# Attention with its inverse sums in the units that turn p, and the end of a layer in passes of parts

## The chip, the cores and the metric

The kernel runs on one core of a Trainium2 chip. The metric is the device time of one execution in microseconds (us). A core has five engines that run side by side and wait for one another by semaphores: TensorE (PE in the profile; PEld is its weight load), VectorE (DVE), ScalarE (ACT), GpSimd (POOL) and SyncE (SP), which issues most transfers.

## The reference, cut to what matters

A graph network on 1250 nodes with 512 features and 40000 edges, four stages one after the other. The change touches the second stage, two layers of attention over edges with 8 heads of 64 features. Of each layer it computes

```
scores = einsum('ehd,ehd->eh', q[tgt], k[srcidx])
m = segment_max(scores, tgt);  p = exp(scores - m[tgt])
s = segment_sum(p, tgt)
w = p / (s[tgt] + 1e-16)
agg = segment_sum(w[:, :, None] * v[srcidx], tgt)
attn = agg.reshape(n, D) @ Wo[l].T + bo[l]
x = _batchnorm(x + attn, g1[l], beta1[l])
ff = relu(x @ W1[l].T + b1[l]) @ W2[l].T + b2[l]
x = _batchnorm(x + ff, g2[l], beta2[l])
```

with Wo 512 by 512, W1 256 by 512 and W2 512 by 256. The batch norm is over the 1250 nodes, for each feature.

## The kernel before, in words

Edges are not walked one by one. Each layer has two blocks of code, `attend` and `finish_layer`, and between blocks the engines meet.

**attend** works on dense tiles: 8 heads times 10 groups of 128 target nodes, 80 steps, each with the 1250 source nodes in a row. What an engine does in step n stands in its own loop, in an order written out by hand; steps are skewed (scores run three steps ahead). In one step PE makes the scores of one tile (6 matmuls, L1337 and L1338, into banks 0 to 2), DVE takes them out and adds the logarithms of the edge counts (L1435, which I call a take), ACT does the exponential and sums it (L1396), PE turns the tile in two units of five 128 by 128 transposes (L1355, banks 4 to 7), ACT and DVE split each unit into a high and a low part (L1404, L1441), and PE multiplies the parts with the values (L1366, L1367, bank 3). The scores have one set of banks, so the scores of the next tile wait for the take of this one. Two heads are a pair, 20 steps; there are four pairs.

After each pair the sum is inverted and spread over 64 columns per head (`invert`, L1451 to L1453, at the end of step 21, 41 and 61), PE transposes the ten blocks of it into the banks of the scores (`spread`, L1345), and DVE multiplies the pair's rows of the result with it out of these banks (`divide`, L1460). For the first three pairs this stands in the middle of the loop, one step after the inversion; for the last one behind it. The list `score_plan` puts the spreads among the scores, and the counter `taken` counts both. GpSimd meanwhile gathers edge features for a later stage, 28 groups per layer (L806, L809).

**finish_layer** loads and turns Wo, W1 and W2 (L1055, ACT copies them out, L1581). `product` (L1556) multiplies: for each of the outputs (512 or 256 features in blocks of 128, times three thirds of 417 nodes) it runs over all input blocks in float32, and four banks go round. DVE adds bias and the old x (L1643); after three thirds it has a block of 128 features complete, takes its mean and variance (L102 to L108), ACT gives the root (L1585), and DVE normalises (L1624 to L1631). Product n waits until sum n-4 is out of its bank. W1 waits at its first output for the blocks of x one by one (`x_ready`), and in layer 0 the weights Wq of the next layer are turned after its second output. ACT applies relu (L1598). W2 starts when all six thirds of the hidden layer are there. In layer 1 GpSimd adds a row to ten tiles as soon as x is normalised (L1530).

The same kernel does another product in three passes already: `project_tensor` (L1142) for q and k of a layer, where both sides are split into a high part that PE takes in its fast float32 format (fp32r) and the rest, and high x high, high x low and low x high are added up.

## Time and profile before

| what | us |
|---|---|
| median of 3 runs (lowest, highest) | 2629.24 (2628.74, 2633.49) |
| the profiled execution | 2624.77 |
| its span in the trace | 2622.6 |
| PE busy | 2421.7 (92%) |
| DVE busy | 2063.6 (79%) |
| ACT busy | 1701.0 (65%) |
| POOL busy | 1087.3 (41%) |

Times in the trace count from the start of the span. Layer 0 has its attend from 808 to 1113 and its finish from 1113 to 1208, layer 1 from 1287 to 1594 and from 1594 to 1682. In a row of the timeline stand: start, busy time, engine, line, operation, output <- input, how many were merged, and in brackets how long the engine was idle before and what ended that. A row of the windows has: stretch, length, then busy time and instructions of PE, PEld, DVE, ACT and POOL, the clock granted to TensorE (1.00 is 2.4 GHz, 0.50 is 1.2 GHz), the share of the DMA engines and GB/s. A group of lines has: line, engine, operation, output <- input, shapes, count | busy us, mean ns of one | idle before.

### The profile page before, as it was taken

To read this page: it belongs to the slowest core of one execution; us is meant where nothing else is said; L and a number is where in the kernel's file an instruction comes from. 1 tells how busy PE (TensorE), PEld (TensorE's weight loads), DVE (VectorE), ACT (ScalarE), POOL (GpSimd) and SP (SyncE) were. 2 spreads that over 40 slices of the span, in tenths; PEclk is the share of its full clock that TensorE was granted. 3 is DMA by queue.
4 is the path that set the end of the run, shared out by engine and by line. 5 is a ranking of instruction groups with operands and counts; after the bars stand their busy time and mean duration, and the time that the engine had idled before them with its cause. 6 is when DMAs were issued, how large, how long until landed. Compare 5 with 4: busy or idle time off the path is not lost. (4 is left out here: it accounts for less than half of the span.)

```text
span 2622.6 us, 44503 instructions
## 1 busy us (share of the span) xinstructions
PE 2421.7 (92%) x12795; PEld 1927.9 (74%) x12795; DVE 2063.6 (79%) x4105; ACT 1701.0 (65%) x3714; POOL 1087.3 (41%) x1059
## 2 busy tenths in 40 slices
PE   6999699998998999999999998788999999988987
PEld 3777455556798999857899995456777777757776
DVE  8789699998646888836498885666999999966767
ACT  1789788886725777614377772242999999945460
POOL 1776655534203544000154420213777777720122
PEclk9999899999999999999899999898999999998999
DMA  2004022213245344112444441113877777841101
GB/s 94 3 3 126 29 66 65 65 43 101 74 176 124 101 113 116 32 65 100 138 120 117 91 79 65 49 56 120 245 235 241 237 238 236 224 122 36 49 9 39
DMA packets 116544, 278.10 MB, mean 106 GB/s; under 512 B 23991, under 2 KB 38266, under 8 KB 116414
## 3 DMA queue, kind: packets, MB, share of 16 engines
q0 software_dynamic: 51328, 138.78, 19.3%
q1 hardware_dynamic: 65086, 137.65, 16.8%
q8 instruction: 73, 1.20, 0.2%
q14 instruction: 57, 0.47, 0.1%
HBM read 208.80 MB, written 59.43 MB: 102 GB/s over the span
## 5 line engine op out<-in xcount | busy, mean ns | idle before, releaser
L806 POOL DMA_INDIRECT feature_rows<-in_edge_attr,id_idx x352 | 341.0, 969 | 448.9 <-POOLq L1507 226.9
L2081 POOL DMA_INDIRECT x_got<-table_dram,src_idx x352 | 375.4, 1066 | 110.0 <-issue 82.6
L1441 DVE TENSOR_TENSOR pt_low<-bank,pt_high 128x640 fp32r<-128x640 f32 x320 | 262.8, 822 | 52.8 <-ACT pt_high L1404 51.6
L761 ACT ACTIVATE hot_rest<-hot_dst,slot_w 128x128 bf16<-128x128 bf16 x864 | 273.1, 400 | 44.1 <-DVE hot_dst L711 44.1
L1404 ACT CAST pt_high<-bank 128x640 fp32r<-128x640 f32 x320 | 219.6, 687 | 114.3 <-PE bank L1355 114.3
L2225 DVE TENSOR_TENSOR msg<-bank,x_got 128x512 f32<-128x512 f32 x352 | 236.9, 684 | 42.6 <-ACT msg_high L2170 15.6
L1435 DVE CUSTOM_DVE_ANT_0 p<-bank,log_counts 128x1254 f32<-128x1254 f32 x160 | 232.6, 1454 | 14.7 <-PE bank L1338 14.5
L1355 PE MATMUL bank<-ident,p 128*128 128x128 f32 x1600 | 229.1, 275 | 2.3 <-DVE pt_low L1441 2.3
L1396 ACT ACTIVATE p<-p,bound 128x1254 f32<-128x1254 f32 x160 | 215.3, 1346 | 9.8 <-DVE bound L1435 9.8
L1366 PE MATMUL bank<-pt_high,val 128*128 128x256 f32 x800 | 212.3, 300 | 0.9 <-DVE agg_t L1447 0.9
L2205 DVE SCALAR_TENSOR_TENSOR msg_low<-msg,msg_high 128x512 fp32r<-128x512 f32 x308 | 209.7, 681 | 0.0
L2170 ACT ACTIVATE msg_high<-msg 128x512 fp32r<-128x512 f32 x308 | 193.4, 628 | 14.6 <-DVE msg L2225 14.2
L217 POOL DMA_INDIRECT slots_dram<-rec,pos x152 | 154.4, 1015 | 113.3 <-issue 102.4
L1367 PE MATMUL bank<-pt_low,val 128*128 128x256 f32 x800 | 199.2, 284 | 0.0
L1355 PEld LDWEIGHTS bank<-ident,p 128*128 128x128 f32 x1600 | 190.7, 142 | 11.4 <-issue 3.2
L1337 PE MATMUL bank<-keys,queries 128*128 128x418 f32 x480 | 186.6, 389 | 12.6 <-DVE bound L1435 7.3
L1338 PE MATMUL bank<-keys,queries_low 128*128 128x418 f32 x480 | 172.7, 360 | 0.0
L782 PE MATMUL bank<-hot_src,hot_rest 128*128 128x417 bf16 x864 | 172.0, 341 | 0.0
L809 POOL DMA_DIRECT2D features_dram<-feature_rows x88 | 51.0, 580 | 275.8 <-DMA feature_rows<-in_edge_attr,id_idx 275.8
L582 PE MATMUL bank<-row_hot,col_part 125*128 125x352 f32 x840 | 157.2, 340 | 8.6 <-ACT col_part L625 4.5
L582 PEld LDWEIGHTS bank<-row_hot,col_part 125*128 125x128 f32 x840 | 135.9, 191 | 29.6 <-issue 20.1
L1366 PEld LDWEIGHTS bank<-pt_high,val 128*128 128x128 f32 x800 | 152.9, 191 | 1.3 <-DVE pt_low L1441 1.3
(439 smaller groups left out, 6336.4 us busy)
## 6 DMA issues: line engine op xcount, KB each, us to landing
features_dram<-feature_rows POOLq DMA_DIRECT2D x88, 256.0 KB
edge_got<-features_dram SPq DMA_DIRECT2D x88, 256.0 KB, 3.7
qk_dram<-qk_high SPq DMA_DIRECT2D x16, 640.0 KB, 2.9
qk_dram<-qk_low SPq DMA_DIRECT2D x16, 640.0 KB, 4.2
keys<-qk_dram SPq DMA_DIRECT2D x32, 320.0 KB, 4.7
queries<-qk_dram SPq DMA_DIRECT2D x32, 320.0 KB, 6.7
queries_low<-qk_dram SPq DMA_DIRECT2D x32, 320.0 KB, 8.7
acc_a<-zeros SPq DMA_DIRECT2D x1, 6400.0 KB, 31.1
```

The source lines that it names most:

```text
L582: m = pe.matmul(ps_p[:, q, :], col_part[0:EP, u, q, :], row_hot[0:EP, u, :], start=(c == 0), stop=(c == PE_COLS - 1))
L761: last = act.activation(hot_rest[:, u, j, q, :], hot_dst[:, u, :, j], ACT.Copy, scale=k.slot_w[:, 1 + q, bass.ds(tile0 + j, 1)])
L806: pool.indirect_dma_start(out=self.rows[:, u, t % GT * ED:(t % GT + 1) * ED], out_offset=None, in_=self.a.edge_attr_128, in_offset=bass.In ...
L1355: t = pe.transpose(unit(i)[:, j * P:(j + 1) * P], p[:, n % AHEAD, (u * HALF + j) * P:(u * HALF + j + 1) * P], k.ident[:])
L1366: pe.matmul(to, v, p_high[:, slot, j, :], start=(u == 0 and j == 0), stop=False)
L1396: act.activation(rows, rows, ACT.Exp, bias=bound[:, n % 4:n % 4 + 1], scale=-1.0, accum_out=sums[:, n // (2 * NB) % 2, n % NB, n // NB % 2 ...
L1404: act.copy(p_high[:, made % 3, :, n % 2 * P:(n % 2 + 1) * P], unit(2 * n + u).rearrange("p (j n) -> p j n", n=P)).then_inc(high_made, 1)
L1435: dve.tensor_tensor_reduce(out=thirds(p[:, n % AHEAD, :]), in0=k.bank[:, 0:3, 0:THIRD], in1=thirds(k.log_counts[:, n % NB, :]), scale=-1.0 ...
L1441: dve.tensor_tensor(p_low[:, made % 3, :, columns], unit(2 * n + u).rearrange("p (j n) -> p j n", n=P), p_high[:, made % 3, :, columns].bi ...
L2081: pool.indirect_dma_start(out=xg[:, g % XRING, j, :], out_offset=None, in_=k.table_dram, in_offset=bass.IndirectOffsetOnAxis(ap=k.src_idx[ ...
L2205: dve.scalar_tensor_tensor(low[:, u, j, :], msg[:, j, :], 0.0, high[:, u, j, :].bitcast(F32), ALU.max, ALU.subtract).then_inc(low_done, 1)
L2225: dve.tensor_tensor(msg[:, j, :], k.bank[:, 2 + j, :], xg[:, r, j, :], ALU.add).then_inc(added_x, 1)
```

## The change

1. In `attend` the inverse sums of the first three pairs no longer go through the banks of the scores. PE transposes them as two further units of five blocks in the ring of units that turns p, one behind step 24 (44, 64) and one behind step 25 (45, 65); ACT copies each to SBUF (`inv_rows`), and GpSimd multiplies the pair's rows with it, between two of its groups of edge features (`SCALED_BEHIND`). The last pair is done as before.
2. In `finish_layer` the products with Wo and W2 take three passes of parts in fp32r instead of one float32 product. ACT rounds the result of attention and the weights to the high part, DVE subtracts to get the low part. The first six outputs of Wo are run input block by input block, over six banks; the other six output by output.
3. W1 stays float32, with its six outputs in six banks, input block by input block. Half of Wq is turned before its last block and half behind it. ACT writes the hidden layer twice (rounded, and whole), DVE subtracts.

```
+SCALED_BEHIND = (30, 53, 76)
...
-        p = (n - (2 * NB + 5)) // (2 * NB)
-        if n >= 2 * NB + 5 and (n - (2 * NB + 5)) % (2 * NB) == 0:
-            plan.append(("spread", p))
-        plan.append(("scores", n))
-    plan.append(("spread", HP - 1))
+        behind = n - 2 * NB - SPREAD_BEHIND
+        for u in range(2):
+            plan.append(("p", n, u))
+            if behind >= 0 and behind % (2 * NB) in (0, 1) and u == 1:
+                plan.append(("inv", behind // (2 * NB), behind % (2 * NB)))
     return plan
...
-            features.gather(pool, GATHERED[l], GATHERED[l + 1])
+            first, end = GATHERED[l], GATHERED[l + 1]
+            for pair in range(HP - 1):
+                until = first + (end - first) * SCALED_BEHIND[pair] // BLOCKS
+                features.gather_groups(pool, first, until)
+                first = until
+                pool.wait_ge(inv_copied, 2 * (pair + 1))
+                pool.wait_ge(batch_added, 2 * HALF * (pair + 1))
+                rows = at.agg[:, pair, :]
+                pool.tensor_tensor(rows, rows, inv_rows[:].rearrange("p u n -> p (u n)"), ALU.mult).then_inc(pair_scaled, 1)
+            features.gather_groups(pool, first, end)
+            features.all_stored(pool, end)
...
+            def unit_free(item):
+                i = turn_of[item]
+                if i >= UNITS:
+                    kind, n, u = turns[i - UNITS]
+                    pe.wait_ge(low_made if kind == "p" else inv_copied, 2 * n + u + 1)
...
+            def turn_inverse(pair, u):
+                pe.wait_ge(inv_ready, pair + 1)
+                unit_free(("inv", pair, u))
+                for j in range(HALF):
+                    t = pe.transpose(unit(("inv", pair, u))[:, j * P:(j + 1) * P], spread_inv(pair)[:, u * HALF + j, :], k.ident[:])
                 t.then_inc(turned, 1)
...
                     turn(n, 0)
-                if n + AHEAD < BLOCKS:
-                    kind, i = next(following)
-                    if kind == "spread":
-                        spread(i)
-                        kind, i = next(following)
                 if n >= 2:
                     values((n - 2) // 2, n % 2)
                 if n < BLOCKS:
                     turn(n, 1)
                 if n + AHEAD < BLOCKS:
-                    scores(i)
+                    scores(n + AHEAD)
+                if n in inverse_behind:
+                    turn_inverse(*inverse_behind[n])
             spread(HP - 1)
...
+            def copy_inverse(pair, u):
+                act.wait_ge(turned, turn_of["inv", pair, u] + 1)
+                if pair:
+                    act.wait_ge(pair_scaled, pair)
+                act.copy(inv_rows[:, u, :], unit(("inv", pair, u))).then_inc(inv_copied, 1)
...
-                if n + AHEAD < BLOCKS:
-                    kind, i = next(following)
-                    if kind == "spread":
-                        divide(i)
-                        kind, i = next(following)
                 if n < BLOCKS:
                     low_part(n, 0)
                 if n >= 3 and n % 2 == 1:
...
-                if n > 1 and n % (2 * NB) == 1:
+                if n > 1 and n % (2 * NB) == INVERTED:
                     invert(n // (2 * NB) - 1)
                 if n + AHEAD < BLOCKS:
-                    take(i)
+                    take(n + AHEAD)
...
-                    if n >= 2:
+                    if 2 <= n < 2 + KC:
+                        pe.wait_ge(w_lowered, n - 1)
+                    elif n >= 2:
                         pe.wait_ge(w_copied, n - 1)
...
+            def rows_of_wo(n, i):
+                to, o, c = out_of(n, RING)
+                for q, s in ((0, 0), (0, 1), (1, 0)):
+                    m = pe.matmul(to, wo[:, q, i, o], agg_parts[s][:, i, c], start=(i == 0 and q + s == 0), stop=(i == KC - 1 and q == 1))
+                return m
 
             turn(0, KC)
-            pe.wait_ge(w_copied, KC)
-            product(wo, at.agg, KC, KC, o_done, o_added, None, lambda: turn(KC, len(turns)), OTHERS)
+            for i in range(KC):
+                pe.wait_ge(w_lowered, i + 1)
+                pe.wait_ge(agg_low_made, i + 1)
+                for n in range(RING):
+                    m = rows_of_wo(n, i)
+                    if i == KC - 1:
+                        m.then_inc(o_done, 1)
+            turn(KC, len(turns))
+            for n in range(RING, 3 * KC):
+                pe.wait_ge(o_added, n - RING + 1)
+                for i in range(KC):
+                    m = rows_of_wo(n, i)
+                m.then_inc(o_done, 1)
             pe.wait_ge(w_copied, len(turns))
-            pe.wait_ge(o_added, 9)
-            product(w1, k.x1t, KC, FP, h_done, h_copied, x_ready, turn_following if following else None, WEIGHTS)
-            pe.wait_ge(h_copied, 3 * FP)
-            product(w2, hid, FP, KC, f_done, f_added)
+            for i in range(KC):
+                if i == KC - 1 and following:
+                    turn_following(0, EARLY)
+                pe.wait_ge(x_ready, i + 1)
+                for n in range(3 * FP):
+                    to, o, c = out_of(n, RING)
+                    if i == 0:
+                        pe.wait_ge(o_added, 3 * KC - RING + n + 1)
+                    m = pe.matmul(to, w1[:, i, o], k.x1t[:, i, c], start=(i == 0), stop=(i == KC - 1))
+                    if i == KC - 1:
+                        m.then_inc(h_done, 1)
+            if following:
+                turn_following(EARLY, KC)
+            pe.wait_ge(w_lowered, len(low_parts))
+            for n in range(3 * KC):
+                if n < 3:
+                    pe.wait_ge(h_low_made, 3 * (FP - 1) + n + 1)
+                if n >= 4:
+                    pe.wait_ge(f_added, n - 3)
+                to, o, c = out_of(n, 4)
+                for i in range(FP):
+                    for q, s in ((0, 0), (0, 1), (1, 0)):
+                        m = pe.matmul(to, w2[:, q, i, o], hid[:, s, i, c], start=(i == 0 and q + s == 0), stop=(i == FP - 1 and q == 1))
+                m.then_inc(f_done, 1)
...
+                    if n < KC:
+                        act.copy(agg_parts[0][:, n, :], at.agg[:, n, :]).then_inc(agg_high_made, 1)
...
-            copies(0, KC)
+            copies(0, len(turns))
             for o in range(KC):
                 root(0, o)
-                if o == 0:
-                    copies(KC, len(turns))
+            if following:
+                for c in range(EARLY):
+                    weight_high(act, k, following, 0, c)
             for n in range(3 * FP):
-                if following and n == WEIGHTS:
-                    for j in range(KC):
-                        weight_high(act, k, following, 0, j)
                 act.wait_ge(h_done, n + 1)
-                c = WIDE[n % 3]
-                act.activation(hid[:, n // 3, c:c + C3], k.bank[:, 2 + n % 4, 0:C3], ACT.Relu,
-                               bias=at.vec[:, at.B1 + n // 3:at.B1 + n // 3 + 1]).then_inc(h_copied, 1)
+                (c, wide), bias = EVEN[n % 3], at.vec[:, at.B1 + n // 3:at.B1 + n // 3 + 1]
+                act.activation(hid[:, 0, n // 3, c:c + wide], k.bank[:, 2 + n % RING, 0:wide], ACT.Relu, bias=bias)
+                if n >= 2:
+                    act.wait_ge(h_low_made, n - 1)
+                act.activation(hid_whole[:, n % 2, 0:wide], k.bank[:, 2 + n % RING, 0:wide], ACT.Relu, bias=bias).then_inc(h_copied, 1)
+            if following:
+                for c in range(EARLY, KC):
+                    weight_high(act, k, following, 0, c)
...
+                    if not turn and n == RING:
+                        for m, to in low_parts[KC:]:
+                            low_part(m, to)
...
+            for i in range(KC):
+                dve.wait_ge(agg_high_made, i + 1)
+                dve.tensor_tensor(agg_parts[1][:, i, :], at.agg[:, i, :], agg_parts[0][:, i, :].bitcast(F32), ALU.subtract).then_inc(agg_low_made, 1)
+                low_part(*low_parts[i])
+            add_and_norm(o_done, o_added, at.BO, at.G1, at.BETA1, 0, RING)
...
+            for n in range(3 * FP):
+                c, wide = EVEN[n % 3]
+                dve.wait_ge(h_copied, n + 1)
+                dve.tensor_tensor(hid[:, 1, n // 3, c:c + wide], hid_whole[:, n % 2, 0:wide], hid[:, 0, n // 3, c:c + wide].bitcast(F32), ALU.subtract).then_inc(h_low_made, 1)
```

How the instructions stand on DVE around the first pair of layer 0 (inv_s and inv_spread are the inverse sums, agg_t is the result of attention, ISA p,bound is the take). Before:

```order
L1441 TENSOR_TENSOR pt_low<-bank,pt_high 128x5x128
L1447 TENSOR_TENSOR agg_t<-bank,pv_rest 64x256
L1441 TENSOR_TENSOR pt_low<-bank,pt_high 128x5x128
L1451 TENSOR_SCALAR inv_s<-sums 128x20
L1452 RECIPROCAL inv_s<-inv_s 128x20
L1453 COPY inv_spread<-inv_s 128x1280
L1435 ISA p,bound<-bank,log_counts 128x1254
L1435 ISA bound 128x1
L1460 TENSOR_TENSOR agg_t<-agg_t,bank 128x1280
L1441 TENSOR_TENSOR pt_low<-bank,pt_high 128x5x128 x2
L1435 ISA p,bound<-bank,log_counts 128x1254
```

And now:

```order
L1490 TENSOR_TENSOR pt_low<-bank,pt_high 128x5x128
L1496 TENSOR_TENSOR agg_t<-bank,pv_rest 64x256
L1490 TENSOR_TENSOR pt_low<-bank,pt_high 128x5x128
L1500 TENSOR_SCALAR inv_s<-sums 128x20
L1501 RECIPROCAL inv_s<-inv_s 128x20
L1502 COPY inv_spread<-inv_s 128x1280
L1484 ISA p,bound<-bank,log_counts 128x1254
L1484 ISA bound 128x1
L1490 TENSOR_TENSOR pt_low<-bank,pt_high 128x5x128 x2
```

The inversion stands where it stood, between the low part and the take; the multiplication of agg_t with the bank is gone from DVE, and nothing has come in its place there.

How ACT begins the end of layer 0 (wo_in and w_in are the turned weights, agg_high the rounded result of attention, bn_dev the root of the batch norm). Before:

```order
L1581 COPY wo_in<-bank 128x512 x4
L1585 ACT_TABLE_LOAD
L1585 ACTIVATE bn_dev<-bn_var 128x1
L1581 COPY w_in<-bank 128x256 x4
L1581 COPY w_in<-bank 128x512 x2
L1585 ACTIVATE bn_dev<-bn_var 128x1 x3
L1598 ACTIVATE hidden<-bank,vec 128x417 x2
L1126 CAST wqkv_a_7132<-bank 128x512 x4
L1598 ACTIVATE hidden<-bank,vec 128x417 x4
```

And now:

```order
L1660 CAST agg_high<-agg_t 128x1280
L1662 CAST wo_in<-bank 128x512
L1660 CAST agg_high<-agg_t 128x1280
L1662 CAST wo_in<-bank 128x512
L1662 COPY w_in<-bank 128x256 x4
L1662 CAST w_in<-bank 128x512 x2
L1666 ACT_TABLE_LOAD
L1666 ACTIVATE bn_dev<-bn_var 128x1 x4
L1135 CAST wqkv_a_7132<-bank 128x512 x2
L1677 ACTIVATE hidden<-bank,vec 128x418
```

Each of the four copies of Wo now has a cast of the result of attention ahead of it (the first three pairs stand above these rows), and all copies of weights stand ahead of the load of the table and of the first root, where there was one root ahead of the copies of W1 and W2.

How PE goes from Wo to W2 in layer 0 (wo_rows and wqkv_rows are weights to be turned, x1t is the normalised x). Before:

```order
L1055 MATMUL bank<-ident,wo_rows_7149 128x128 x16
L1556 MATMUL bank<-agg_t,wo_in 128x417 x16
L1055 MATMUL bank<-ident,wo_rows_7147 128x128 x8
L1055 MATMUL bank<-ident,wo_rows_7148 128x128 x8
L1556 MATMUL bank<-agg_t,wo_in 128x417 x32
L1556 MATMUL bank<-x1t,w_in 128x417 x8
L1055 MATMUL bank<-ident,wqkv_rows_a_7127 128x128 x16
L1556 MATMUL bank<-x1t,w_in 128x417 x16
L1556 MATMUL bank<-hidden,w_in 128x417 x24
```

And now, from the last input block but one of W1 on:

```order
L1631 MATMUL bank<-x1t,w_in 128x418 x2
L1631 MATMUL bank<-x1t,w_in 128x416
L1064 MATMUL bank<-ident,wqkv_rows_a_7127 128x128 x8
L1631 MATMUL bank<-x1t,w_in 128x418 x2
L1631 MATMUL bank<-x1t,w_in 128x416
L1631 MATMUL bank<-x1t,w_in 128x418 x2
L1631 MATMUL bank<-x1t,w_in 128x416
L1064 MATMUL bank<-ident,wqkv_rows_a_7127 128x128 x8
L1645 MATMUL bank<-hidden,w_in 128x418 x12
L1645 MATMUL bank<-hidden,w_in 128x416 x6
```

W1 was 8 matmuls (two outputs of four blocks), then all of Wq, then 16; now six matmuls of one input block stand together, half of Wq is turned ahead of the last such six and half behind them, and W2 has three times as many matmuls per output.

## Rows read from the trace of the kernel before

**Rows 1.** Windows, a steady stretch of attention in layer 0

```profile
850.00:880.00 30.00, 30.00 (x229) 29.47 (x229) 27.54 (x42) 24.47 (x39) 13.39 (x16) 1.00 0.36 102
```

**Rows 2.** Timeline, takes of steps 6, 22, 79 (layer 0), then 6 and 79 (layer 1)

```profile
831.70 1.45 DVE L1435 CUSTOM_DVE_ANT_0 p<-bank,log_counts 128x1254 f32<-128x1254 f32 x1
...
886.52 1.45 DVE L1435 CUSTOM_DVE_ANT_0 p<-bank,log_counts 128x1254 f32<-128x1254 f32 x1
...
1096.22 1.45 DVE L1435 CUSTOM_DVE_ANT_0 p<-bank,log_counts 128x1254 f32<-128x1254 f32 x1
...
1312.02 1.45 DVE L1435 CUSTOM_DVE_ANT_0 p<-bank,log_counts 128x1254 f32<-128x1254 f32 x1
...
1577.31 1.45 DVE L1435 CUSTOM_DVE_ANT_0 p<-bank,log_counts 128x1254 f32<-128x1254 f32 x1
```

**Rows 3.** Timeline, the first pair's inverse sums in layer 0

```profile
893.96 1.04 DVE L1453 COPY inv_spread<-inv_s 128x1280 f32<-128x1280 f32 x1
...
894.92 1.45 DVE L1435 CUSTOM_DVE_ANT_0 p<-bank,log_counts 128x1254 f32<-128x1254 f32 x1
...
896.52 1.28 PE L1345 MATMUL bank<-ident,inv_spread 128*128 128x128 f32 x10 [2.96 <-DVE bound L1435]
...
897.91 1.49 DVE L1460 TENSOR_TENSOR agg_t<-agg_t,bank 128x1280 f32<-128x1280 f32 x1 [1.54 <-PE bank L1345]
...
899.45 0.46 PE L1337 MATMUL bank<-keys,queries 128*128 128x418 f32 x1
```

**Rows 4.** Windows, behind the second pair's spread; at the head of finish_layer

```profile
969.20:972.70 3.50, 3.46 (x20) 3.49 (x21) 1.80 (x2) 0.00 (x0) 2.11 (x3) 0.63 0.24 85
...
1116.00:1117.00 1.00, 1.00 (x7) 0.79 (x5) 0.00 (x0) 0.65 (x2) 0.00 (x0) 0.55 1.02 373
```

**Rows 5.** Timeline of an earlier stage, GpSimd beside DVE

```profile
653.71 2.93 POOL L873 TENSOR_TENSOR count_low<-acc_c,count_high 128x1280 fp32r<-128x1280 f32 x1 [4.04 <-ACT count_high L929]
...
655.01 2.97 DVE L990 TENSOR_TENSOR log_counts<-counts_above,log_counts 128x1280 f32<-128x1280 f32 x1
...
659.51 1.47 DVE L990 TENSOR_TENSOR log_counts<-counts_above,log_counts 128x1280 f32<-128x1280 f32 x1
...
663.03 3.79 POOL L873 TENSOR_TENSOR count_low<-acc_c,count_high 128x1280 fp32r<-128x1280 f32 x1 [6.39 <-ACT count_high L929]
...
663.89 0.75 DVE L999 SCALAR_TENSOR_TENSOR alpha<-bank,inv,alpha 128x512 f32<-128x512 f32 x1
```

**Rows 6.** Timeline, weights turned for Wo and the first sum, layer 0

```profile
1113.59 3.58 PE L1055 MATMUL bank<-ident,wo_rows 128*128 128x128 f32 x16 [1.92 <-PEq L1308]
...
1120.96 0.65 DVE L1643 SCALAR_TENSOR_TENSOR x1t<-bank,vec,x1t 128x417 f32<-128x417 f32 x1 [7.69 <-PE bank L1556]
```

**Rows 7.** Timeline, float32 matmuls of Wo; outputs of q in three passes

```profile
1131.89 22.57 PE L1556 MATMUL bank<-agg_t,wo_in 128*128 128x417 f32 x64
...
1225.88 0.61 ACT L1199 ACTIVATE qk_whole<-bank,bq 128x418 f32<-128x418 f32 x1 [1.68 <-PE bank L1142]
...
1228.12 0.61 ACT L1199 ACTIVATE qk_whole<-bank,bq 128x416 f32<-128x416 f32 x1 [1.63 <-PE bank L1142]
```

**Rows 8.** Lines by form, a cast on ACT and a low part on DVE

```profile
L929 ACT CAST count_high<-acc_c 128x1280 fp32r<-128x1280 f32 x9 | 11.3, 1266 | 19.4 <-PE bank L902 19.4
...
L1133 DVE TENSOR_TENSOR wqkv_a<-bank,wqkv_a 128x512 fp32r<-128x512 f32 x16 | 10.6, 686 | 12.5 <-ACT wqkv_a L1126 12.5
```

**Rows 9.** Timeline, W1 waits for x; statistics and first root of W2's norm

```profile
1159.26 3.77 PE L1556 MATMUL bank<-x1t,w_in 128*128 128x417 f32 x10 [2.70 <-DVE x1t L1631]
...
1183.28 1.58 DVE L102 BATCH_NORM_STATS2 bn_pieces<-x1t 128x6 f32<-128x417 f32 x3
...
1185.35 0.20 ACT L1585 ACTIVATE bn_dev<-bn_var 128x1 f32<-128x1 f32 x1 [7.14 <-DVE bn_var L108]
...
1663.24 0.20 ACT L1585 ACTIVATE bn_dev<-bn_var 128x1 f32<-128x1 f32 x1 [7.32 <-DVE bn_var L108]
```

**Rows 10.** Timeline, GpSimd in the end of layer 1

```profile
1640.40 12.27 POOL L1530 TENSOR_TENSOR x_rows<-x_rows,ln_b_row 128x512 f32<-128x512 f32 x10 [84.61 <-DVE x1t L1631]
```

More of the change, by code:

```diff
@@ L799, in gather, with gather_groups @@
     def gather(self, pool, first, end):
+        self.gather_groups(pool, first, end)
+        self.all_stored(pool, end)
+    def gather_groups(self, pool, first, end):
         for g in range(first, end):
@@ L1285, in attend @@
     place = {item: i for i, item in enumerate(plan)}
+    turns = turn_plan()
+    turn_of = {item: i for i, item in enumerate(turns)}
     steps = BLOCKS + 2
+    inverse_behind = {turns[i - 1][1]: item[1:] for i, item in enumerate(turns) if item[0] == "inv"}
     def thirds(rows):
@@ L1368, in values @@
                 x.then_inc(half_done, 1)
[L1370 to L1372 removed]
+            for n in range(AHEAD):
+                scores(n)
             for n in range(steps):
@@ L1544, in turn_following @@
                     turn_weight(pe, k, following, 0, c)
-            def product(w, x, inputs, outputs, done, free, arrive=None, others=None, at_n=None):
-                for n in range(3 * outputs):
-                    o, c = n // 3, WIDE[n % 3]
-                    if others and n == at_n:
-                        others()
-                    if n >= 4:
-                        pe.wait_ge(free, n - 3)
-                    for i in range(inputs):
-                        if arrive and n == 0:
-                            pe.wait_ge(arrive, i + 1)
-                        m = pe.matmul(k.bank[:, 2 + n % 4, 0:C3], w[:, i, o * P:(o + 1) * P], x[:, i, c:c + C3],
-                                      start=(i == 0), stop=(i == inputs - 1))
-                    m.then_inc(done, 1)
@@ L1617, in _, with low_part, add_and_norm @@
             me = Steps(nc, dve, at.sem("finish_dve"))
-            def add_and_norm(done, added, bias, gain, beta, turn):
+            def low_part(n, to):
+                dve.wait_ge(w_copied, n + 1)
+                dve.tensor_tensor(to, k.bank[:, n % 2, :], turns[n][3].bitcast(F32), ALU.subtract).then_inc(w_lowered, 1)
+            def add_and_norm(done, added, bias, gain, beta, turn, ring):
                 def normalise(o):
```

85 lines of the change are left out of this document (50 added, 35 removed).

## The prediction

> **What bounds the kernel now.** I read the windows first. In attention PE is busy 30.00 of 30.00 us at full clock, DVE 27.54 [rows 1]: PE sets the pace. The timeline of the takes gives the period: step 6 to step 22 is 54.82 us for 16 steps, 3.43 us each [rows 2]. DVE is near it, 92% busy.
>
> Then the timeline around a pair. The inverse sums use the banks of the scores, and that breaks the skew. PE idles 2.96 us until the take at 894.92 is out, transposes for 1.28 us, DVE multiplies from 897.91 for 1.49 us, and the scores start at 899.45 [rows 3]. From the end of that take (896.5) to the scores it is 2.95 us. The inversion ahead of it pushed the take back by 1.3 to 1.5 us (its copy alone took 1.04).
>
> What all six inner pairs cost together comes from the outer takes. Layer 0: 1096.22 - 831.70 = 264.52 us for 73 steps; 73 x 3.427 = 250.2; rest 14.3. Layer 1: 1577.31 - 1312.02 = 265.29; rest 15.1 [rows 2]. Sum 29.4 us, 4.9 a pair. That is more than 1.4 + 2.95, since behind some pauses the clock falls: granted 0.63 in the 3.5 us behind the second pair's pause [rows 4], and its matmuls take almost twice as long.
>
> In the end of a layer one float32 matmul is two rows of PE, 64 of them in 22.57 us, so 0.705 us per product of blocks [rows 7]. PE bounds Wo and W1 except for 2.70 us in which it waits for x [rows 9]. In W2 DVE bounds (statistics, sums and the low parts of x).
>
> **Attention, part by part.** What goes: the 2.95 us between take and scores, and the pause that lets the clock fall. What stays: the inversion, at its place, with nothing on PE to cover it, since scores wait for the take: the same 1.3 to 1.5 us, of which I take 1.35. What is added on PE: ten transposes per pair, 0.12 us apart, 1.2 us in two halves of 0.6, on the engine that bounds. Would their waits add more? A unit waits for the one two before it. For the unit behind the inverse this is ACT's copy of it. ACT takes as long for it as for a unit of p, 0.69 us (219.6 us for 320 on the page), behind the exponential; it ends about 2.9 us after the scores of that step began, and PE comes to that unit after 3.65 (scores 1.23, inverse 0.6, unit 0.6, values 1.2). So nothing waits, ACT is 82% busy [rows 1] and takes two copies more per pair. After: 1.35 + 1.2 = 2.55 a pair, 15.3 for six. **Attention gains 29.4 - 15.3 = 14.1 us.** Bounds: if the two copies and GpSimd's waits cost a stall of 0.6 for each unit, 12 x 0.6 = 7.2 less, 7; if the take's delay is partly covered, 16.
>
> GpSimd's multiplication: 2.93 us for the same form [rows 5], three per layer, beside a gather that ended 84.6 us before 1640.40, at 1555.8, while attention of layer 1 went on to 1592 [rows 10]. Three times 3, and some 10 us of waiting for the first pair's copies, end it near 1580, where attention after the change ends at 1585. Cost nothing, with little to spare; without this cover up to 3 us in layer 1.
>
> The multiplication also runs beside DVE. The rows of an earlier stage tell which operations suffer: one with two inputs in SBUF takes 2.97 us while GpSimd's subtraction runs and 1.47 us without; one that reads a bank and one tile takes 0.75 us beside a GpSimd operation [rows 5]. All DVE operations of the attention loop but the inversion read a bank. So I take nothing.
>
> The Trainium skill, "SBUF — State Buffer", section "Who interferes with whom", says that a DVE instruction with two SBUF inputs contends with a GpSimd instruction that reads SBUF and that one with at most one does not. By that rule attention is safe as well, and the end of layer 1 is not (below); the trace agrees.
>
> **The end of layer 0.** I go along PE's queue.
> - Head. Before, the first matmul of Wo could start after 16 transposes (3.58 us from 1113.59 [rows 6]). Now PE turns block 3 only when DVE has lowered block 1. DVE needs ACT's first cast (1.27), then twice a low part of the result (1.49) and of the weight (0.69) [rows 3, 8]: 1.3 + 4.36, with gaps 5.8 us. Then 4 transposes at half clock (granted 0.55 at 1116 [rows 4]), 0.9: the passes start at about 1120.3, 2.5 us later than now.
> - Six outputs by input block. A pass takes 0.19 us: 12 matmuls of q took 1228.12 - 1225.88 = 2.24 us [rows 7], so a block product takes 0.57 and not 0.705. 72 passes are 13.5 us. Before, the clock was up again when PE had turned the last of its 16 blocks; now pauses lie between the transposes, and I let it rise only within the first input block of passes, half of which (9 of 18) then take 0.38 instead of 0.19: 1.7 us. End 1135.6. Bounds: 0 and all of it at half clock (13.5).
> - Turning W1 and W2: 3.0 us, as before, to 1138.6. Six outputs of 2.27 us: 1152.2, against 1131.89 + 22.57 = 1154.4 [rows 7]. Gain 2.2.
> - W1. 24 x 0.70 = 16.8 us, half of Wq 1.0 and 0.9 us of waiting for sums: 1171.0. Before, W1 ended at 1177.4, with the 2.70 us for x [rows 9], turning Wq with stalls for ACT and DVE (3.5), and the same 16.8. DVE has x ready at about 1160.7 (it waits for the root, that now stands behind the table load of 1.28 us), and its last block is wanted at 1166.8. Gain now 6.4.
> - W2. ACT writes the hidden layer twice, 12 operations of the form that takes 0.61 us alone [rows 7] and some 0.52 where they follow at once: 6.3 us from 1167.6, to 1173.9; DVE then lowers the last third and two blocks of Wq, 2 us: first sum at 1175.9. But three sums now stand ready, 3 x 0.62, and statistics 2.07 (1185.35 - 1183.28 [rows 9]): first root at 1179.9, against 1185.35. **Gain 5.5 us.** From there DVE bounds, as before, and W2's saving on PE (24 x 0.13 = 3 us) buys nothing.
>
> **The end of layer 1.** The same, without Wq: first root at 1658.2 against 1663.24 [rows 9], 5.0 us. But GpSimd's ten additions run for 12.27 us from the normalised x on [rows 10], about 1641.6 to 1654, and the six low parts of the hidden layer (two SBUF inputs, 0.6 us each) fall into 1648 to 1654. Four of them meet an addition of 1.23 us: 3 us at most, 0 at least. I take 2.5, since the rows show that such a pair of operations takes the sum of both. **Gain 2.5 us.**
>
> **Sum.** 14.1 + 5.5 + 2.5 = 22.1 us. Against its own time: 2624.77 - 22.1 = 2602.7 for a profiled execution. The median of the runs lies 4.5 us above the profiled one, so 2629.24 - 22.1 = **2607 us**.
>
> **The rivals.**
> - The end of a layer gives nothing: DVE and ACT have 20 operations more there, DVE has a chain of its own through Wo (sums, statistics and normalising, some 5.7 us per 128 features against 6.8 of PE), and if the first root and the low parts of W2 put x behind 1166.8, W1 waits again. For it: DVE's 28 us from first sum to last x are one waiting chain; against: 6 us of room. Time 2629 - 14 = 2615.
> - Attention gives half: a stall per inverse unit (7.2). For it: DVE at 92% beside PE at 100%, and the inversion's delay moves low parts too. Time 2614.
> - More than forecast: no late clock (+1.7 twice), no contention (+2.5), part of the inversion covered (+2): 2599.
> - GpSimd's multiplication stops DVE: 6 x 3 = 18 us, and the gain is 4: 2625, no change. Against it stands the 0.75 us row.
> - **Slower:** TensorE's clock stays at 1.2 GHz in Wo. The place is the head: four short groups of transposes with pauses between them, then passes. A pass then takes 0.38; all 144 of a layer cost 27 us more, both layers 54, time 2629 - 25 + 54 = 2658. It decides once over 116 passes more than I count run at the low level (22.1 / 0.19). For it: the clock is at 0.50 to 0.55 there now [rows 4]; against: it rose within the transposes, and the passes leave PE no pause.
>
> The Trainium skill, "TensorE: Matmul & The Clock Gate", section "HAM oscillation — how this bites in real kernels", holds that idle gaps between bursts of matmuls throttle the clock again, so that the burst behind each runs at half rate. By it the pauses at the head work against the change and the removed pauses in attention for it; the trace agrees at the second pair.
>
> **How the numbers follow.** Forecast 0.52, nothing at the layer's end 0.15, half in attention 0.10, more 0.15, DVE stopped 0.04, clock low 0.04 (slower). I leave out the last two: from 2598 to 2620. A difference under 0.2%, 5.3 us, counts as no change. Faster: the first four, 0.92; same 0.04; slower 0.04.
>
> **What would show it.** Steps per pair: takes 24 and 44 still 1.3 to 1.5 us late, then two steps of 4.0 us and no pause of 2.9; granted clock 1.00 all through attention. Outer takes of a layer 73 x 3.43 + 7.6 = 257.8 us apart. Wo: 12 passes in 2.27 us; its last output 2 us earlier than now, counted from the block's start. First root of W2's norm 5.5 us (layer 0) and 2.5 us (layer 1) earlier in its block. Low parts of the hidden layer 0.6 us in layer 0 and over 1 us in layer 1. I am wrong if scores still wait for more than a take, if DVE's low parts in attention grow past 0.82 us, or if x is late for W1.

## The result, and the profile after

The changed kernel takes 2602.6 us (median of 4 runs, 2600.1 to 2607.8) against 2629.0 of the kernel before: ratio 0.9902, 95% interval 0.9888 to 0.9915. The medians lie 26.4 us apart; the forecast was 2607, 22.1 less. The profiled execution took 2600.13 us; its span went from 2622.6 to 2598.3, 24.3 us less, and the ledger below divides these.

Takes of the changed kernel, the timeline (start, duration, engine, line): steps 6 and 79 of layer 0, then of layer 1.

```profile
831.43 1.45 DVE L1484 CUSTOM_DVE_ANT_0 p<-bank,log_counts 128x1254 f32<-128x1254 f32 x1
...
1089.93 1.45 DVE L1484 CUSTOM_DVE_ANT_0 p<-bank,log_counts 128x1254 f32<-128x1254 f32 x1
...
1296.49 1.46 DVE L1484 CUSTOM_DVE_ANT_0 p<-bank,log_counts 128x1254 f32<-128x1254 f32 x1
...
1555.03 1.46 DVE L1484 CUSTOM_DVE_ANT_0 p<-bank,log_counts 128x1254 f32<-128x1254 f32 x1
```

They lie 258.50 and 258.54 us apart where they lay 264.52 and 265.29 [rows 2]. The steps around the first pair, timeline of the changed kernel:

```profile
904.25 0.71 PE L1400 MATMUL bank<-ident,inv_spread 128*128 128x128 f32 x5
904.77 1.45 DVE L1484 CUSTOM_DVE_ANT_0 p<-bank,log_counts 128x1254 f32<-128x1254 f32 x1
905.00 0.74 PE L1393 MATMUL bank<-ident,p 128*128 128x128 f32 x5
...
908.47 0.71 PE L1400 MATMUL bank<-ident,inv_spread 128*128 128x128 f32 x5
908.98 1.46 DVE L1484 CUSTOM_DVE_ANT_0 p<-bank,log_counts 128x1254 f32<-128x1254 f32 x1
909.21 0.74 PE L1393 MATMUL bank<-ident,p 128*128 128x128 f32 x5
...
910.21 2.97 POOL L1343 TENSOR_TENSOR agg_t<-agg_t,inv_rows 128x1280 f32<-128x1280 f32 x1 [11.93 <-ACT inv_rows L1451]
```

The five transposes of an inverse unit (L1400) stand between units of p. No pause opens on PE beside them, but they take PE's time: two steps last 4.21 us (904.77 to 908.98, and to 913.19) instead of 3.43. The pause of 2.96 us [rows 3] is gone. GpSimd's last multiplication of layer 1 and the end of its gather:

```profile
1548.71 2.99 POOL L1343 TENSOR_TENSOR agg_t<-agg_t,inv_rows 128x1280 f32<-128x1280 f32 x1
...
1560.89 0.58 POOL L814 DMA_DIRECT2D features_dram<-feature_rows  x1 [4.26 <-DMA feature_rows<-in_edge_attr,id_idx]
1617.04 3.71 POOL L1580 TENSOR_TENSOR x_rows<-x_rows,ln_b_row 128x512 f32<-128x512 f32 x3 [55.58 <-DVE x1t L1719]
```

The gather ends at 1561.5, attention at 1571.7: 10 us to spare.

The end of layer 0 in the changed kernel (timeline):

```profile
1107.68 1.94 PE L1064 MATMUL bank<-ident,wo_rows 128*128 128x128 f32 x8 [1.91 <-PEq L1332]
1111.10 1.11 PE L1064 MATMUL bank<-ident,wo_rows 128*128 128x128 f32 x4 [1.47 <-DVE wo_in L1705]
1113.10 1.11 PE L1064 MATMUL bank<-ident,wo_rows 128*128 128x128 f32 x4 [0.89 <-DVE wo_in L1705]
1113.86 0.70 PE L1605 MATMUL bank<-agg_high,wo_in 128*128 128x418 f32 x1
...
1161.08 0.60 DVE L1760 TENSOR_TENSOR hidden<-hidden_whole,hidden 128x418 fp32r<-128x418 f32 x1 [0.38 <-ACT hidden_whole L1680]
...
1164.82 7.43 PE L1645 MATMUL bank<-hidden,w_in 128*128 128x418 f32 x38 [0.54 <-DVE hidden L1760]
...
1171.65 0.20 ACT L1666 ACTIVATE bn_dev<-bn_var 128x1 f32<-128x1 f32 x1 [4.46 <-DVE bn_var L108]
```

Counted from the block's first transpose, the first pass starts at 6.18 us (in the kernel before the float32 matmuls of Wo started at 4.26), and the first root of W2's norm (ACT's first bn_dev behind W2) comes at 63.97 instead of 71.76 [rows 6, 9]. In layer 1:

```profile
1625.30 6.41 DVE L1760 TENSOR_TENSOR hidden<-hidden_whole,hidden 128x418 fp32r<-128x418 f32 x5 [0.40 <-ACT hidden_whole L1680]
...
1636.61 0.20 ACT L1666 ACTIVATE bn_dev<-bn_var 128x1 f32<-128x1 f32 x1 [6.35 <-DVE bn_var L108]
```

The block starts at 1571.69, so the root stands at 64.92 instead of 68.74. The row merges five low parts: one by one they take 1.18, 1.65, 1.65, 1.67 and 0.58 us, where one took 0.60 in layer 0. The four long ones each meet one of GpSimd's additions, the last stands behind them; and these additions take 1.61 to 1.64 us where they take 1.26 alone.

The ledger of the 24.3 us: attention, between the outer takes, 6.0 and 6.75; end of layer 0 to the first root 7.8; end of layer 1 3.8; start of attention in layer 1 1.85; the rest together -1.9 (all that stands behind the last norm of layer 1 took 942.9 us instead of 940.6). The 1.85 us are TensorE's clock. Windows over the slow stretch at the start of layer 1's attention (stretch, length, then PE, PEld, DVE, ACT, POOL busy, granted clock), changed kernel:

```profile
1276.80:1283.70 6.90, 5.33 (x16) 4.49 (x17) 1.99 (x3) 2.86 (x4) 1.85 (x2) 0.51 1.04 227
```

and kernel before:

```profile
1287.50:1301.20 13.70, 10.52 (x32) 9.02 (x33) 5.53 (x8) 5.79 (x8) 4.57 (x6) 0.50 0.75 163
```

No edit touches these steps. From the first scores of layer 1 on, the slow clock lay on 13.7 us in the kernel before and on 6.8 in the changed one. In the nine traces from chips of the same speed, the stretch from the last root of layer 0 to the take of step 6 in layer 1 goes with this length: 110.7 us where it is 13.7 (before, attend_only), 109.4 to 109.6 where it is 10.2 (end_only, w1_whole, wo_f32, best), 108.8 where it is 6.8 (changed, pool_late, split_later). Why it is shorter in one than in another is open.

### The profile page after: what moved, and what is told of

The parts are those of the page before. It is cut to its first block and busy times, and to the rows that moved or that the text cites. A ratio compares the mean times of both kernels' runs of the same rounds, so it can differ in the third digit from the quotient of the medians.

```text
span 2598.3 us, 44879 instructions
## 1 busy us (share of the span) xinstructions
PE 2407.6 (93%) x12939; PEld 1954.0 (75%) x12939; DVE 2084.7 (80%) x4131; ACT 1724.1 (66%) x3746; POOL 1107.5 (43%) x1065
## 5 line engine op out<-in xcount | busy, mean ns | idle before, releaser
L1484 DVE CUSTOM_DVE_ANT_0 p<-bank,log_counts 128x1254 f32<-128x1254 f32 x160 | 232.9, 1456 | 13.7 <-PE bank L1372 13.3
L1412 PEld LDWEIGHTS bank<-pt_low,val 128*128 128x128 f32 x800 | 152.1, 190 | 0.0
```

The source lines that it names most:

```text
L1412: x = pe.matmul(to, v, p_low[:, slot, j, :], start=False, stop=(u == 1 and j == HALF - 1))
L1484: dve.tensor_tensor_reduce(out=thirds(p[:, n % AHEAD, :]), in0=k.bank[:, 0:3, 0:THIRD], in1=thirds(k.log_counts[:, n % NB, :]), scale=-1.0 ...
```

## The experiments

The table has, from one trace of each kernel, in us from the block's first transpose and for layer 0 / layer 1: when the granted clock rises to 1.00, the end of Wo's last output, and the first root of W2's norm; then the time against the kernel before on the same chip, with its 95% interval. early_passes, w2_f32, split_inverse and dve_multiplies ran on a chip on which the kernel before takes 2825.6 us; there attention has late steps of its own, so only ratios and single steps are used of them.

| kernel | clock up | Wo's end | first root | ratio |
|---|---|---|---|---|
| before | 3.3 / 3.7 | 40.9 / 41.0 | 71.8 / 68.7 | 1 |
| changed | 8.9 / 9.1 | 37.7 / 37.8 | 64.0 / 64.9 | 0.9902 (0.9888 to 0.9915) |
| attend_only | 9.3 / 4.2 | 43.4 / 41.0 | 74.3 / 68.7 | 0.9952 (0.9938 to 0.9966) |
| end_only | 11.4 / 10.2 | 38.8 / 38.3 | 65.1 / 66.3 | 0.9957 (0.9941 to 0.9973) |
| w1_whole | 10.2 / 9.2 | 38.3 / 37.8 | 71.4 / 68.9 | 0.9943 (0.9926 to 0.9961) |
| wo_f32 | 3.1 / 3.9 | 39.9 / 40.3 | 65.8 / 65.7 | 0.9909 (0.9891 to 0.9926) |
| early_passes | 8.8 / 8.6 | 37.1 / 36.9 | 63.3 / 66.4 | 0.9908 (0.9878 to 0.9938) |
| w2_f32 | 9.5 / 9.7 | 37.9 / 38.0 | 63.5 / 61.9 | 0.9875 (0.9854 to 0.9897) |
| pool_late | 9.0 / 9.4 | 37.7 / 37.9 | 64.0 / 63.0 | 0.9897 (0.9877 to 0.9918) |
| split_later | 8.6 / 10.4 | 37.6 / 38.4 | 63.8 / 66.5 | 0.9882 (0.9863 to 0.9901) |
| best | 8.5 / 8.1 | 36.9 / 36.7 | 62.5 / 60.6 | 0.9855 (0.9836 to 0.9874) |

Of the variants of the changed kernel only w1_whole (slower) and best (faster) have intervals clear of its own. What the others say rests on their traces.

**attend_only**: the changed kernel with finish_layer of before. 

> The change in attention alone (the layer's end as before). Theory, from the traces of before and after: the six inner pairs give 12.8 us (takes of step 6 and 79 lie 6.0 and 6.75 us closer), nothing else moves: 258.5 us between these takes in both layers, about 2615 us against 2629, ratio 0.995. Rival 1: most of the whole gain of 26 us comes from here, because a later start of the layer's end had hidden something: under 2608. Rival 2: the halves need each other (GpSimd's multiplications leave the gather late for the float32 layer's end): over 2620.

2617.2 us. Takes 258.25 and 258.20 us apart. **end_only**: the kernel before with the changed finish_layer. 

> The change in the layer's end alone (attention as before). Theory: first root of the second norm 7.8 us earlier in layer 0 and 3.8 in layer 1, counted from the first transpose of the block; 11.6 us in all, about 2617 us, ratio 0.9955. The 1.85 us between the end of q in layer 1 and its take of step 6 (clock 0.53 there before, 0.70 after) come only if the clock falls the same way again. Rival: the gain of layer 1 was the clock's or the gather's, then first root of layer 1 is less than 3 us earlier and the time over 2620.

2617.8 us. Both times are as forecast, and the halves add up: 0.9952 x 0.9957 = 0.9909. But the first roots come 6.65 and 2.4 us earlier, not 7.8 and 3.8, so the first condition of the second rival (layer 1 under 3 us) came true. Two things explain it: the clock rises 2.4 and 1.1 us later in its blocks than in those of the changed kernel, which costs 1.1 and 0.5 us at Wo's end, and in layer 1 it takes 0.9 us more from W1's end to the root (below). The layer's end of attend_only is instruction for instruction that of before, yet in layer 0 Wo ends 2.5 us later. Windows at its head in attend_only:

```profile
1111.40:1114.00 2.60, 2.54 (x4) 1.47 (x5) 0.00 (x0) 1.29 (x2) 0.00 (x0) 0.50 1.00 362
1114.00:1117.00 3.00, 3.00 (x6) 1.43 (x6) 0.04 (x1) 0.00 (x0) 0.00 (x0) 0.61 0.14 47
```

The clock rises 9.3 us behind the first transpose here; in the kernel before after 3.3, ahead of the first matmul of Wo. So with the same instructions the rise moved Wo's end by 2.5 us, and a difference of that size in one layer's end isn't by itself the work of an edit. Over all kernels it isn't chance alone: with float32 in Wo the rise came at 3.1 to 4.2 us in five of six blocks, with the passes at 8.1 to 11.4 in every block. The late clock goes with the new head.

**w1_whole** (the edit, shortened to the order of the loops)

```diff
-            for i in range(KC): ... for n in range(3 * FP): one matmul
+            for n in range(3 * FP): ... for i in range(KC): one matmul
```

> The changed kernel, but W1 output by output again (four blocks of input behind each other, the early half of the next Wq behind two outputs), Wo and W2 in three passes. Theory: Wo now ends 7.6 us before the last block of x is ready, and W1 by chunks fills that time. Without it the tensor engine waits for x more than 5 us in each layer (2.70 before the change) and, as the hidden layer is then written while W1 runs, the first root of W2's norm comes about 4 us later per layer: some 8 us more than the changed kernel, about 2611. Rival: the chunks save only the 2.7 us that were waited before, less what the late writing of the hidden layer costs, and the time is within 2 us of the changed kernel.

2614.3 us. PE in its end of layer 0:

```profile
1147.23 0.97 PE L1631 MATMUL bank<-x1t,w_in 128*128 128x418 f32 x2 [0.90 <-DVE x1t L1718]
1152.41 6.44 PE L1631 MATMUL bank<-x1t,w_in 128*128 128x418 f32 x10 [4.21 <-DVE x1t L1718]
```

PE waits 5.1 us in each layer, and the first roots come 7.4 and 4.0 us later: the layer's end then gains 0.4 and -0.1 us over the kernel before. The theory holds, its size in layer 0 was too small, since the waiting has a second price. Windows behind the longer wait:

```profile
1151.10:1157.80 6.70, 5.39 (x8) 2.86 (x9) 1.78 (x4) 1.11 (x2) 0.00 (x0) 0.50 0.01 2
```

The clock was down for the first 5.4 us of W1's work, about 2.7 us of loss. (In the kernel before it stayed up behind the wait of 2.70 us.) The passes without the chunks only turned PE's work into waiting for x. The opposite, W1 by chunks with Wo and W2 both in float32, was not run.

**wo_f32** (shortened; the casts and low parts for Wo are left out too)

```diff
-                for q, s in ((0, 0), (0, 1), (1, 0)):
-                    m = pe.matmul(to, wo[:, q, i, o], agg_parts[s][:, i, c], ...)
+                return pe.matmul(to, wo[:, i, o], at.agg[:, i, c], ...)
```

> The changed kernel, but Wo as float32 matmuls on the whole values again, six outputs by input block; W1 by chunks and W2 in three passes stay. The eight casts and low parts of the attention result and of Wo are gone. Theory: the passes save 48 x 0.13 = 6.2 us of the tensor engine per layer and their head costs 1.9 (first pass 6.2 us after the first transpose against 4.3) and 1.3 for the clock: Wo ends 3 us later without them and the first root of W2's norm too, about 2609. Rival 1: head and clock eat the whole saving, the time is that of the changed kernel, 2603. Rival 2: x is late anyway and W1 absorbs the difference: 2603 as well, but with Wo's end 3 us later and a wait in W1.

2605.1 us. Wo ends 2.2 and 2.5 us later, the roots 1.85 and 0.7. The intervals overlap, so the time alone shows no difference. The traces put the truth between theory and first rival: the first float32 matmul starts 3.3 us behind the first transpose in layer 0, where the clock is up at 3.1; the first pass starts at 6.2 and runs at half rate to 8.9, which costs 1.4 us. Of the 6.2 us that the passes were to save a third is left.

**early_passes**

```diff
-            turn(0, KC)
+            turn(0, 2)
             for i in range(KC):
 ...
+                if i + 2 < KC:
+                    turn(i + 2, i + 3)
```

> The changed kernel, but only two blocks of Wo are turned before the passes of the first input block start; blocks 2 and 3 are turned behind the first and the second input block. Theory: the passes need only the low parts of block 0 (ready 3.4 us after the block's start) but start at 6.2 behind four turns that wait for low parts; started at 3.4, they fill the 2.4 us in which the tensor engine idles, and the engine without pauses is granted the full clock sooner: Wo's end and the first root 1.5 to 2.5 us earlier in each layer, about 2599. Rival: the passes then run at 1.2 GHz for as much longer as they start earlier (0.38 instead of 0.19 us each), and Wo ends at the same time, 2603.

The passes start at 3.41, 2.8 us earlier, but Wo ends only 0.6 and 0.9 us earlier than in the changed kernel. Windows:

```profile
1207.40:1210.00 2.60, 2.57 (x7) 2.47 (x8) 2.60 (x3) 1.13 (x1) 0.00 (x0) 0.50 1.03 364
1210.00:1213.00 3.00, 3.00 (x10) 2.86 (x10) 0.77 (x1) 0.00 (x0) 0.00 (x0) 0.53 0.44 163
1213.00:1216.00 3.00, 3.00 (x19) 2.93 (x19) 0.88 (x2) 1.75 (x2) 0.00 (x0) 1.00 0.00 0
```

PE is busy from 3.4 us on at 1.2 GHz, and the clock rises 8.8 us behind the first transpose (the mean of 0.53 puts it near the end of the second window); in the changed kernel, which idles 2.4 us there, it rose at 8.9. What starts earlier runs at half rate: the rival is nearly right. The ratio shows no gain, and the first root of layer 1 comes 1.5 us later, behind a longer contention with GpSimd (below).

**w2_f32** (shortened)

```diff
-                act.activation(hid[:, 0, ...], ...)
-                act.activation(hid_whole[:, n % 2, ...], ...)
+                act.activation(hid[:, n // 3, ...], ...)
-                    for q, s in ((0, 0), (0, 1), (1, 0)): (W2, and the six low parts on DVE)
+                    m = pe.matmul(to, w2[:, i, o], hid[:, i, c], ...)
```

> The changed kernel, but W2 as float32 matmuls on the whole hidden layer, which ScalarE writes once; its six low parts on VectorE are gone. Wo in passes and W1 by chunks stay. Theory: behind W1 ScalarE's second writing and the low parts are on the path, and VectorE bounds W2 anyway, so the three passes there cost time: first root of W2's norm 0.4 us earlier in layer 0 (the next Wq's turn covers most) and 2.2 us in layer 1, where GpSimd's additions stretch the low parts from 0.6 to over 1.2 us; 2600. Rival: three outputs at 1.41 us instead of 1.14 bring the third sum 0.8 us later and the rest is hidden: time as that of the changed kernel or 1 to 2 us more.

Ratio 0.9875 on the slower chip, where the changed kernel itself was not run; first roots 0.4 and 3.05 us earlier than in its trace. By these the theory holds: the passes of W2 cost more than they save. Of the 3.05 us in layer 1 some 2 are the contention that pool_late takes away.

**pool_late**

```diff
-            pool.wait_ge(x_ready, KC)
+            pool.wait_ge(h_low_made, 3 * FP)
```

> The changed kernel, but in the end of layer 1 GpSimd's ten additions wait until the six low parts of the hidden layer are made. Theory: VectorE's low parts (two operands in SBUF) and GpSimd's additions hinder each other; alone a low part takes 0.59 us as in layer 0, the first root of W2's norm comes 1.3 us earlier (from the end of W1 9.99 us in layer 1 against 8.41 in layer 0, of which layer 0 has 1.28 for the next Wq). Nothing else is late: the additions (12.3 us) end before the stage behind needs its rows. Rival: the low parts are that long because the hidden layer's writing holds them; they stay at over 1 us.

2604.4 us. VectorE and GpSimd in its layer 1, timeline:

```profile
1629.43 0.59 DVE L1760 TENSOR_TENSOR hidden<-hidden_whole,hidden 128x416 fp32r<-128x416 f32 x1 [0.40 <-ACT hidden_whole L1680]
...
1630.17 9.97 POOL L1580 TENSOR_TENSOR x_rows<-x_rows,ln_b_row 128x512 f32<-128x512 f32 x8 [67.84 <-DVE hidden L1760]
...
1634.63 0.20 ACT L1666 ACTIVATE bn_dev<-bn_var 128x1 f32<-128x1 f32 x1 [5.23 <-DVE bn_var L108]
...
1635.26 1.22 DVE L1712 TENSOR_TENSOR bn_scale<-bn_dev,vec 128x1 f32<-128x1 f32 x1
1636.52 1.21 DVE L1713 TENSOR_TENSOR bn_shift<-bn_mean_var,bn_scale 128x1 f32<-128x1 f32 x1
1637.76 1.18 DVE L1714 TENSOR_TENSOR bn_shift<-vec,bn_shift 128x1 f32<-128x1 f32 x1
1638.98 1.83 DVE L1719 TENSOR_SCALAR x1t<-x1t,bn_scale,bn_shift 128x1251 f32<-128x1251 f32 x1
```

The low parts take 0.59 us and the first root comes 1.95 us earlier: the contention is shown. But the last root of the block comes 2.1 us later than in the changed kernel (83.1 against 81.05 from the first transpose), since now the three small operations of the norm (0.16 us each elsewhere) and the normalising (1.83 instead of 0.93) meet the additions. "Nothing else is late" was wrong, and the time shows no gain.

**dve_multiplies**: VectorE does the six multiplications (same operation, three steps behind the turned inverse). 

> The changed kernel, but VectorE multiplies the six inner pairs by the inverse rows (both operands in SBUF), three steps later than the inversion's transposes, and GpSimd does not. Theory: VectorE is 92% busy beside a tensor engine at 100%, so an operation of 1.49 us delays a take by 1.2: 7 us over both layers, about 2610. Rival: the three tiles of p ahead cover it, and GpSimd's multiplication is worth nothing: 2603.

Ratio 0.9907 (0.9873 to 0.9940), which decides nothing. The trace does:

```profile
1158.15 1.48 DVE L1504 TENSOR_TENSOR agg_t<-agg_t,inv_rows 128x1280 f32<-128x1280 f32 x1
1159.55 1.46 DVE L1480 CUSTOM_DVE_ANT_0 p<-bank,log_counts 128x1254 f32<-128x1254 f32 x1
```

This step lasts 4.82 us, the next three 2.97, 3.75 and 3.43: 1.25 us more than four steps of 3.43. Three of the six pairs have just this; at the others a late step of that chip mixes in. Six times 1.25 would be 7.5 us, near the 7 of the theory; as a whole time it isn't shown.

**split_inverse**

```diff
+PIECE_AT = {2: (0, 3), 3: (3, 5), 4: (5, 8), 5: (8, 10)}
-                dve.tensor_copy(spread_inv(pair)..., inv[:, pair % 2]...)   (one copy at step 1)
+                if n > 2 * NB and n % (2 * NB) in PIECE_AT: spread_piece(...)
```

> The changed kernel, but the copy that spreads the inverse over 128 x 1280 is cut into four pieces, one in each of the four steps behind the inversion. Theory: the whole copy (0.83 to 1.04 us) stands in front of one take and the tensor engine waits for that take: 1.5 or 1.3 us at the take and 0.3 at the next. VectorE has 0.27 us to spare in a step, so the pieces of about 0.25 hide: 1.1 us less a pair, takes of steps 6 and 79 255.2 us apart instead of 258.5, about 6.6 us in both layers, 2596. Rival: what delays is the wait for the sums and the two small operations (0.5 us), or the pieces cost more than they hide; under 2 us less, 2601 or more.

Ratio 0.9897, no gain to be seen. The step before take 24 and its like, 4.7 to 5.0 us in the changed kernel, lasts 3.9 to 4.1, but the last piece came too late:

```profile
1000.24 0.28 DVE L1505 COPY inv_spread<-inv_s 128x256 f32<-128x256 f32 x1
1000.44 1.46 DVE L1485 CUSTOM_DVE_ANT_0 p<-bank,log_counts 128x1254 f32<-128x1254 f32 x1
...
1000.58 0.77 PE L1401 MATMUL bank<-ident,inv_spread 128*128 128x128 f32 x5 [0.71 <-DVE inv_spread L1505]
```

PE waits 0.7 to 0.9 us for it at each pair. **split_later** has SPREAD_BEHIND = 6. 

> The changed kernel with the inverse spread in four pieces, as in the first trial with pieces, but turned two steps later. There the last piece stood behind the turn that needed it (a wait of 0.7 us, take 29 0.48 us later than without pieces). Theory: with that wait gone take 24 is 0.6 to 1.0 us less late than in the changed kernel and takes 30 and 31 keep 4.2 us each: outer takes of a layer 256 us apart against 258.5, about 5 us in all, ratio 0.988. Rival: the turned units cost more where they stand now, the outer takes stay 258 apart.

2600.8 us, ratio 0.9882 (0.9863 to 0.9901); outer takes 256.6 apart in both layers, 1.9 less than in the changed kernel, 3.9 us in all of the 5 forecast. A pair now costs 2.1 to 2.3 us over steady steps instead of 2.7 to 2.9; the two small operations of the inversion stay in front of the take. As a whole time the gain isn't shown: the span is that of the changed kernel (2598.6 against 2598.3), as the first root of layer 1 comes 1.5 us later and what stands behind the last norm takes 945.6 us instead of 942.9.

**best** joins split_later, early_passes and w2_f32. 

> The changed kernel with three edits: the inverse is spread in four pieces and turned two steps later (behind 6 and 7 instead of 4 and 5), the passes of Wo start behind two turned blocks, and W2 is float32 with the hidden layer written once. From the traces of the single edits, against the changed kernel: pieces 0.8 us a pair, 5 us; passes started early 0.9 a layer, 1.8; W2 0.4 and 3 us. Sum 10 us, about 2592 where the kernel before takes 2629, ratio 0.986. Rival: the single gains were the clock's phase at the head of the layer's end and single late steps; then the ratio stays at 0.989 or more.

2593.6 us (2592.8 to 2595.6) where about 2592 was forecast. Its interval ends below that of the changed kernel; they ran on separate occasions, each against the kernel before. Outer takes 256.66 and 256.48, first roots 1.5 and 4.3 us earlier than in the changed kernel. It has the lowest ratio of all, though its interval overlaps that of w2_f32.

## Why the prediction was right, point by point

- **Attention** (14.1 forecast, 12.8 measured, 13.4 in attend_only). The inversion costs 1.4 us at the first pair of a layer (steps of 4.97, 2.96 and 3.75) and about 1.1 at the others (4.69), where 1.35 was taken; in attend_only it is 1.1 at all six. The two inverse units cost 0.78 each, not 0.6; this term was mis-sized by 0.36 a pair. Together 2 x 1.4 + 4 x 1.1 + 12 x 0.78 = 16.6 us, which is what the outer takes show, against 15.3. What was saved depends also on the execution of the kernel before: three of its six pauses brought the clock down, with a step of 7.6 to 7.7 us behind the late take instead of 6.1; in end_only only two did. That no unit waits for another held, and so did the price of GpSimd at nothing (low parts 0.82 us as before). The clock was 1.00 only from 11.4 us behind the first scores of layer 0 on, and from 10.0 in layer 1. GpSimd's end was put at 1580 and was 1561.5: too little cover was assumed.
- **End of layer 0** (5.5; 7.8 here, 6.65 in end_only). The 2.3 us more are three small terms: Wo's end at 37.7 where 38.6 was said (first pass at 6.18 and not 6.7, and 1.4 us for the clock and not 1.7), no wait for sums (0.9 had been added), and 8.25 us from W1's end to the root where the sum had 8.9. 12 passes in 2.27 held. W1 never waited for x: the last x stood ready at 45.1 and was wanted at 51.3, the 6 us of room that had been said. What the sum did not say is where the gain sits: w1_whole shows that without W1 by chunks 0.4 us of it are left. The rival "x is late" had the mechanism, and the chunks are the reason why it didn't come.
- **End of layer 1** (2.5; 3.8 here, 2.4 in end_only). The contention was real, and four low parts met an addition, as forecast. Without it the block gains 5.8 us (pool_late; 5.0 forecast), with it 3.8, so it costs 2.0 here where 2.5 was taken. The price moves with how the two engines meet: from W1's end to the first root it is 10.0 us here, 8.6 in wo_f32, 10.9 in end_only and split_later, 12.3 in early_passes, and 7.9 in pool_late, so 0.7 to 4.4 us, which goes past the bound of 3 that the prediction gave. That low parts would take over 1 us held.
- **"W2's saving on PE buys nothing"** was too kind: by the traces of w2_f32 the passes cost 0.4 and 3 us, ScalarE's second writing and the low parts being on the path.
- **Operations with one SBUF input.** The prediction says that they don't contend with GpSimd. In pool_late the normalising, with one tensor and two single columns from SBUF, took 1.83 us instead of 0.93 beside an addition; the condition that was left out stands in the last section. In attention no run shows such a loss.
- **The clock in Wo** (the slower rival) didn't stay low. These windows of the changed kernel show the head, and where it rose:

```profile
1110.50:1113.90 3.40, 1.92 (x9) 1.52 (x9) 3.40 (x4) 3.36 (x5) 0.00 (x0) 0.50 1.01 351
1113.90:1116.40 2.50, 2.50 (x9) 2.40 (x8) 2.50 (x4) 0.68 (x2) 0.00 (x0) 0.50 0.47 179
1116.40:1119.00 2.60, 2.60 (x15) 2.56 (x15) 0.64 (x2) 0.00 (x0) 0.00 (x0) 0.97 0.01 1
```

- **What the prediction lacked** is the clock at the start of layer 1's attention, 1.85 us, which no edit touches. attend_only has none of it, end_only 1.25, the other variants on chips of that speed 1.0 to 1.9. Against it stand 2.3 us lost behind the last norm of layer 1, a stretch that takes 940.6 to 946.1 us over the nine traces; its cause is open.
- **Luck.** The mechanisms were right and the total came near partly because errors cancel: attention gave 1.3 us less than forecast, the ends of the two layers 2.3 and 1.3 more, the start of layer 1 1.85 more and the rest 1.9 less. That makes the 24.3 us of the traces; another 2 of the 26.4 between the medians is scatter of the runs.

## What to carry to other kernels

When a matmul is made cheaper, look at what its successor waits for: here three passes without the chunked W1 gained next to nothing at the layer's end, and the order of accumulation was worth 11 us on top of them, part of it through a clock that no pause brings down. Splitting into high and low parts pays where the operands lie ready early (Wo, a little) and costs where the split itself is on the path (W2). A broadcast copy in front of the operation that sets the pace can go in pieces into the slack of several steps, if the last piece stands ahead of its reader.

## What the runs showed of the hardware

- A VectorE operation with two inputs in SBUF doesn't just slow down beside a GpSimd operation on SBUF, it waits for it: even one of 128x1 took 1.22 us instead of 0.16, beginning with an addition of 1.28 us and ending with it (pool_late). The additions suffer too, 1.61 to 1.64 us instead of 1.26 beside low parts (changed kernel). The Trainium skill, "SBUF — State Buffer", section "Who interferes with whom", names this pair, and clears an operation with one SBUF input only outside the 2-port modes; the prices are these runs'. Operations that read a bank (sums, 0.65) were not touched.
- The same instructions at the end of layer 0 took 2.5 us more or less by when the granted clock went from 0.50 to 1.00: 9.3 us behind the first transpose in attend_only, 3.3 in the kernel before. With the passes it was 8.1 to 11.4 us in every kernel.
- A wait of 4.2 us on PE was followed by 6.8 us at 0.50 (w1_whole), one of 2.70 us at the same place by none (kernel before). Of the six pauses of 2.7 to 3.0 us in attention of the kernel before, three were followed by 3.4 us at 0.50 and three by none.
